# Macaron block with mixture of experts and windowed attention: both ends of the program anew (small weights turned by TensorE, loads in order of use, gates of the two outer passes spread by TensorE, idle matmuls in TensorE's waits there)

## The reference

```python
def ffn(X):                                   # on layernorm(x)
    shared = silu(X @ sW1 + sb1) @ sW2 + sb2  # 256 -> 128 -> 256
    logits = X @ routing_W.T + expert_bias    # 8 experts
    act = sqrt(softplus(logits))
    cf = the two largest of act in each row, 0 elsewhere
    hdn = silu(einsum('nd,edh->enh', X, rW1) + rb1[:, None])
    y = einsum('enh,ehd->end', hdn, rW2) + rb2[:, None]
    return shared + einsum('ne,end->nd', cf, y)
def attn(X):                                  # 16 heads of 16 channels
    q, k, v = heads(X @ Wq), heads(X @ Wk), heads(X @ Wv)
    # each token sees itself and the 63 before it
    return merge(softmax(q . k_window / 4) . v_window) @ Wo
x = x + 0.5 * ffn(layernorm(x))
x = x + attn(layernorm(x))
x = x + 0.5 * ffn(layernorm(x))
```

## Time and profile before

| | |
|---|---|
| time, median of 3 runs | 1589.93 us (1588.89 to 1590.38) |
| profiled execution, its own time | 1584.86 us |
| its span | 1583.1 us |
| mean granted clock of TensorE | 0.973 |
| TensorE busy | 1479.5 us, 93% |
| VectorE, ScalarE, POOL busy | 75%, 71%, 49% |

### The profile page before, as it was taken

How to read it: one execution, slowest core, us unless ns; L and a number is a source line. 1 busy time by engine, 2 the same in 40 slices (tenths; PEclk the granted TensorE clock), 3 DMA queues, 4 the chain that set the end, 5 groups by cost and what they waited for, 6 DMA issues and landing times.

```text
span 1583.1 us, 40702 instructions
## 1 busy us (share of the span) xinstructions
PE 1479.5 (93%) x13632; PEld 1333.7 (84%) x13632; DVE 1179.6 (75%) x4771; ACT 1128.6 (71%) x3400; POOL 779.8 (49%) x789
## 2 busy tenths in 40 slices
PE   2888999999999999999999999999999999998967
PEld 1777889898898989899898989989898988987756
DVE  5747677878878787887878787787878788675643
ACT  3358686877878687777878677787868778766823
...
GB/s 116 64 164 106 174 111 177 121 125 137 122 172 95 192 110 138 129 124 161 121 181 102 155 128 116 157 124 180 95 176 121 126 138 107 173 82 161 82 20 67
DMA packets 269957, 203.86 MB, mean 129 GB/s; under 512 B 154379, under 2 KB 224421, under 8 KB 269749
## 3 DMA queue, kind: packets, MB, share of 16 engines
...
q10 hardware_dynamic: 3408, 0.02, 0.1%
...
## 4 chain that ended last, share of the span: by engine, by line
PE 85%; DVE 5%; issue 3%; SPq 2%; DMA 2%; POOL 1%; ACT 1%; ACTq 0%; POOLq 0%; DVEq 0%
PE gb L937 12%; PE gb L939 11%; PE gb L938 11%; PE yb L937 9%; PE yb L939 8%; PE yb L938 8%; PE ptb L1000 7%; PE sb_ L991 6%; PE cxb L1019 4%; PE gb L1029 2%; PE gb L1041 2%; PE gb L1039 2%; PE gb L947 1%; SPq L479 1%; PE yb L1073 1%
## 5 line engine op out<-in xcount | busy, mean ns | idle before, releaser
L563 POOL TENSOR_TENSOR gl<-ag,gh 128x512 fp32r<-128x512 f32 x288 | 379.9, 1320 | 240.3 <-ACT gh L661 239.7
L546 POOL TENSOR_TENSOR pr<-pr,rinv 128x512 f32<-128x512 f32 x256 | 272.2, 1064 | 300.2 <-DVE rinv L822 298.3
L617 ACT ACTIVATE pr<-pr,mx 128x128 f32<-128x128 f32 x1024 | 397.5, 395 | 9.7 <-DVE mx L814 7.0
L937 PE MATMUL yb<-w2h,gh 128*128 128x256 f32 x1152 | 336.8, 292 | 12.4 <-POOL gl L563 12.3
L938 PE MATMUL yb<-w2h,gl 128*128 128x256 f32 x1152 | 324.0, 281 | 0.0
L939 PE MATMUL yb<-w2l,gh 128*128 128x256 f32 x1152 | 324.0, 281 | 0.0
L669 ACT ACTIVATE tt<-gb,b1half 128x512 f32<-128x512 f32 x288 | 195.4, 683 | 153.3 <-PE gb L939 147.7
L814 DVE CUSTOM_DVE_ANT_0 pr<-sb_,mask 128x128 f32<-128x128 f32 x1024 | 235.2, 285 | 53.8 <-issue 34.5
L881 DVE SCALAR_TENSOR_TENSOR ag<-gb,b,gate 128x512 f32<-128x512 f32 x256 | 188.2, 744 | 83.0 <-ACT tt L669 63.2
L661 ACT ACTIVATE gh<-ag 128x512 fp32r<-128x512 f32 x288 | 180.7, 628 | 95.1 <-DVE ag L887 66.8
L937 PE MATMUL gb<-xh,w1h 128*128 128x512 f32 x576 | 243.4, 423 | 2.6 <-DVE ag L881 2.0
...
## 6 DMA issues: line engine op xcount, KB each, us to landing
gate<-gates_pair SPq DMA_DIRECT2D x256, 256.0 KB, 3.7
ks<-qk_dram SPq DMA_DIRECT2D x256, 128.0 KB, 3.0
qs<-qk_dram SPq DMA_DIRECT2D x512, 64.0 KB, 2.6
...
```

Source lines behind the costliest of these rows:

```text
L546: nc.gpsimd.tensor_tensor(pr[:, k], pr[:, k], rinv[:, k, :].unsqueeze(2).to_broadcast([P, NP, P]), ALU.mult).then_inc(a_pn, 1)
L563: nc.gpsimd.tensor_tensor(gl[:, k, :], ag[:, k, :], gh[:, k, :].bitcast(F32), ALU.subtract).then_inc(f_gl, 1)
L617: nc.scalar.activation(pr[:, k, r, :], pr[:, k, r, :], ACT.Exp, bias=mx[:, k, r:r + 1], scale=-1.0, accum_out=rsum[:, k, r:r + 1]).then_in ...
L937: nc.tensor.matmul(dst, ah, bh, start=start, stop=False, **kw)
```

## The change

It has six parts.

1. *Small weights.* The router weights and first-layer biases come in rows, contiguous, to a tile `small` (in the tile that later holds `x2`), and three TensorE transposes (`Wt`) turn them. VectorE and ScalarE read the result from PSUM.
2. *Loads.* The order of the loads is changed, `1r` and `2r` are split by halves into `1r`, `1t` and `2r`, `2t`, the raw tiles are others, and POOL does not wait for the transfer of its mask any more.
3. *Clearing.* `Wz` goes from VectorE to POOL, behind the second `gl`.
4. *Gates of pass p of block 0 and of pass q of block 15.* A matmul `B` with a selector column spread over 128 columns writes an expert's gates to all partitions of a PSUM bank (`sb_` or `ptb`), and ScalarE copies them to `gate` (`K`). `cr`, `G1` and the eight `sp` are not run in these passes.
5. *Idle matmuls.* `Z24` is 24 products of the identity with itself, written to `cxb` and read by nobody. 159 such stand in TensorE's table at both ends.
6. *Tables.* `HEAD` now reaches from block 0 to 3, `TAIL` starts at block 10, and `ORDER` is changed between `qH2` and `pH0`. It has the same steps as before.

```diff
@@ step tables, start and end of TensorE's lists @@
 HEAD = {
     "PE": """
-pX0=0 pX1=0 pL=0 pH0=0 pC=0 pY0=0 pH1=0 pH2=0 pH3=0 pH4=0 pH5=0 pY1=0 pH6=0 pY2=0 pH7=0 pY3=0 pH8=0 pY4=0
+Wt=0 Z24=0 pX0=0 pX1=0 Z6=0 pL=0 pH0=0 pH1=0 pH2=0 Z19=0 pC=0 Z2=0 pB0=0 pB1=0 Z3=0 pB2=0 pH3=0 pB3=0 pB4=0
+pY0=0 pH4=0 pB5=0 pB6=0 pY1=0 pH5=0 pB7=0 pH6=0 pY2=0 pY3=0 pH7=0 pH8=0 pY4=0 pY5=0 pX0=1 pX1=1 pY6=0 pY7=0
+pL=1 pH0=1 pY8=0 Z29=1 pY0=1 aX0=0 aX1=0 Z4=1 pC=1 Z2=0 Q00=0 Q01=0 V0=0 pH1=1 pH2=1 Q10=0 Q11=0 V1=0 pY1=1
...
     "POOL": """
-prs=0 prs=1 pzz0=0 pgl0=0 pgl1=0 pgl2=0 pgl3=0 pgl4=0 pgl5=0 pgl6=0 pgl7=0 pgl8=0 pzz0=1 rsa=0 pgl0=1 prs=2
+prs=0 pzz0=0 pgl0=0 pgl1=0 Wz=0 pgl2=0 pgl3=0 prs=1 pgl4=0 pgl5=0 pgl6=0 pgl7=0 pgl8=0 rsa=0 pgl0=1 pzz0=1
...
     "SP": """
-LX=0 LX=1 LW2r=0 LW2s=0 LWvo=0 LW1s=0 LWqk=0 LW1r=0 LWb2=0 pG1=0 psp0=0 psp1=0 psp2=0 psp3=0 psp4=0 psp5=0
+LX=0 LW1s=0 LW1r=0 LW2s=0 LW2r=0 LX=1 LWb2=0 LWvo=0 LWqk=0 LX=2 pG1=1 psp0=1 psp1=1 psp2=1 psp3=1 QW0=0
@@ @@
+        small = x2.rearrange("p t d -> p (t d)")[0:NE, 0:KC * P + HID]
+        turned = sb_[:, :, :].rearrange("p r k -> p (r k)")
+        by_pe = {("p", 0), ("q", B - 1)}
+        def spread_to(m):
+            return sb_[:, :, :].rearrange("p r k -> p (r k)") if m % 2 == 0 else ptb[:]
@@ POOL @@
+            select(sel32[:], ALU.not_equal, 1.0, -32, [[-1, E]], 1)
+            select(sel32[:], ALU.not_equal, 1.0, -40, [[-1, E]], 1)
             pool.dma_start(mask[WIN:2 * WIN, :, :], mask[0:WIN, :, :]).then_inc(w_mask, 16)
-            pool.wait_ge(w_mask, 16)
+                if s == "Wz":
+                    nc.gpsimd.memset(qs[:].bitcast(F32), 0.0).then_inc(w_zero, 1)
+                    pool.wait_ge(w_lo, max(lo_done("1r"), lo_done("1t")))
+                    nc.gpsimd.memset(va[:], 0.0).then_inc(w_zero, 1)
@@ ScalarE @@
-            for c in range(KC):
-                act.dma_start(rwf[:, c, :], routing_w[:, c * P:(c + 1) * P].rearrange("e p -> p e"),
-                              allow_slow_non_contiguous=True).then_inc(w_in[0], 16)
+            act.dma_start(small[0:E, 0:KC * P], routing_w).then_inc(w_small, 16)
+            act.dma_start(small[0:1, KC * P:], sb1.rearrange("(a p) -> a p", a=1)).then_inc(w_small, 16)
+            act.dma_start(small[1:NE, KC * P:], rb1).then_inc(w_small, 16)
...
+                elif s[1] == "K":
+                    n, m = nth(s, b), int(s[2])
+                    act.wait_ge(f_gpe, E * (s[0] == "q") + m + 1)
+                    wait(act, f_a, NE * (n - 1) + m + 6 if m < 4 else NE * n + m - 2)
+                    nc.scalar.activation(gate[:, m % 4, :], spread_to(m), ACT.Copy).then_inc(f_gk, 1)
@@ VectorE @@
-                        dve.wait_ge(f_gate[m], 32 * n + 16 * ((e - 1) // 4) + 16)
+                        if (s[0], b) in by_pe:
+                            dve.wait_ge(f_gk, E * (s[0] == "q") + e)
+                        else:
+                            dve.wait_ge(f_gate[m], 32 * ns(s, b) + 16 * ((e - 1) // 4) + 16)
@@ TensorE @@
+                if s[0] == "Z":
+                    for _ in range(int(s[1:])):
+                        nc.tensor.matmul(cxb[:, 0:2, :].rearrange("p w q -> p (w q)"), ident[:], ident[:], start=True, stop=True)
+                elif s == "Wt":
+                    pe.wait_ge(w_small, 48)
+                    for c in range(KC):
+                        nc.tensor.transpose(turned[:, c * E:(c + 1) * E], small[0:E, c * P:(c + 1) * P], ident[0:E, 0:E])
+                    nc.tensor.transpose(turned[:, KC * E:KC * E + NE], small[:, KC * P:], ident[0:NE, 0:NE]) \
+                        .then_inc(w_smt, 1)
...
+                elif s[1] == "B":
+                    n, m = nth(s, b), int(s[2])
+                    if m == 0:
+                        pe.wait_ge(w_sel, 1)
+                        pe.wait_ge(f_cth, n + 1)
+                    if m > 1:
+                        pe.wait_ge(f_gk, E * (s[0] == "q") + m - 1)
+                    nc.tensor.matmul(spread_to(m), sel[:, m:m + 1].to_broadcast([P, P]), cft[:], start=True, stop=True) \
+                        .then_inc(f_gpe, 1)
```

More of the change, by code:

```diff
@@ new lines @@
+pH5=2 S0=1 pY2=2 pY3=2 S1=1 qX0=0 qX1=0 S2=1 P0=1 qL=0 S3=1 pH6=2 P1=1 pH7=2 S4=1 P2=1 pH8=2 U1=1 qH0=0 S5=1
+P3=1 pY4=2 U3=1 S6=1 pY5=2 P4=1 S7=1 pY6=2 P5=1 pY7=2 qC=0 U5=1 S8=1 P6=1 S9=1 P7=1 pY8=2 U7=1 qH1=0 qH2=0
+qH3=0 pX0=3 qY0=0 pX1=3 P8=1 S10=1 qY1=0 S11=1 aX0=2 aX1=2 pL=3 S12=1 qY2=0 Q00=2 Q01=2 qY3=0 P9=1 qH4=0
+P10=1 U9=1 S13=1 qH5=0 qH6=0 P11=1 Q10=2 S14=1 qH7=0 P12=1 U11=1 S15=1 qY4=0 V0=2 P13=1 qH8=0 P14=1 Q11=2
+qY5=0 P15=1 qY6=0 pH0=3 qY7=0 S0=2 qY8=0 pC=3 U13=1 U15=1 S1=2 V1=2 pY0=3 S2=2 P0=2 O0=1 S3=2 pH1=3 P1=2
@@ new lines @@
+Q01=12 pL=13 qH5=10 qY4=10 qH6=10 Q10=12 P12=11 qH7=10 V0=12 qH8=10 qY5=10 qY6=10 pC=13 P13=11 Q11=12 pH0=13
+P14=11 U13=11 S0=12 qY7=10 P15=11 qY8=10 S1=12 U15=11 V1=12 S2=12 pY0=13 P0=12 O0=11 S3=12 pH1=13 P1=12
+O1=11 S4=12 pH2=13 U1=12 pH3=13 S5=12 P2=12 pY1=13 pH4=13 pH5=13 P3=12 qX0=11 pY2=13 qX1=11 S6=12 U3=12
+pY3=13 P4=12 S7=12 qL=11 pY4=13 pY5=13 pH6=13 pH7=13 P5=12 pH8=13 qH0=11 U5=12 S8=12 P6=12 pY6=13 qC=11
+P7=12 S9=12 pY7=13 qH1=11 pY8=13 S10=12 qH2=11 pX0=14 U7=12 P8=12 S11=12 qY0=11 pX1=14 P9=12 qH3=11 qH4=11
@@ new lines @@
+pY7=14 pY8=14 S10=13 P7=13 qH1=12 qH2=12 pX0=15 S11=13 qY0=12 P8=13 qH3=12 U7=13 P9=13 pX1=15 qY1=12 aX0=14
+S12=13 P10=13 U9=13 qY2=12 aX1=14 qH4=12 P11=13 S13=13 qY3=12 Q00=14 Q01=14 S14=13 P12=13 pL=15 qH5=12
+qY4=12 qH6=12 P13=13 Q10=14 S15=13 P14=13 qH7=12 U11=13 qY5=12 V0=14 Q11=14 qH8=12 qY6=12 pC=15 pH0=15 S0=14
+P15=13 qY7=12 S1=14 U13=13 U15=13 V1=14 qY8=12 S2=14 P0=14 pH1=15 O0=13 pY0=15 S3=14 P1=14 O1=13 U1=14 S4=14
+P2=14 pH2=15 pH3=15 pH4=15 P3=14 pY1=15 S5=14 pH5=15 pH6=15 qX0=13 pY2=15 S6=14 qX1=13 U3=14 P4=14 pY3=15
@@ L171 @@
+qsp5=14 qsp6=14 qsp7=14 OUT=14 OUT=15
 """,
@@ L355, in split, with ns @@
             return pa[:, 2:4].rearrange("p w k n -> p (w k n)"), x1[1].rearrange("p t d -> p (t d)")
+        by_pe = {("p", 0), ("q", B - 1)}
+        def ns(s, b):
+            return sum(x not in by_pe for x in passes[:nth(s, b)])
         def wait(eng, s, value):
@@ L365, in run @@
             apart_ = set(head + tail)
+            apart_ |= {(x + k, b) for x, b in by_pe for k in ["G1", "cr"] + ["sp%d" % m for m in range(E)]}
             for s, b in head:
@@ L467, in step @@
                     c, hf = int(s[2]), int(s[3])
+                    if b == 0 and c == 0:
+                        sp.wait_ge(w_zero, 5)
                     if hf == 0:
@@ L631, in step @@
                     act.wait_ge(f_rstd, 4 * n + 4)
-                    wait(act, f_g1, 16 * n)
+                    wait(act, f_g1, 16 * ns(s, b))
                     src = xin[b % NXI] if s[0] == "p" else x2
@@ L1050, in step @@
                     mm.then_inc(f_ct, 1)
+                elif s[1] == "B":
[7 more added lines that the diff above has]
+                        .then_inc(f_gpe, 1)
                 elif s[1] == "H":
                     e, n, q = int(s[2]), nth(s, b), "pq".index(s[0])
-                    weights("1s" if e == 0 else "1r", n == 0 and e < 2)
+                    weights("1s" if e == 0 else "1r" if e == 1 else "1t", n == 0 and e in (0, 1, 1 + E // 2))
                     if e == 0:
@@ L1063, in step @@
                     k = (NE * n + e) % NG
-                    weights("2s" if e == 0 else "2r", n == 0 and e < 2)
+                    weights("2s" if e == 0 else "2r" if e == 1 else "2t", n == 0 and e in (0, 1, 1 + E // 2))
                     pe.wait_ge(f_gl, NE * n + e + 1)
```

385 lines of the change are left out of this document (223 added, 162 removed).

## The result

The changed kernel takes 1565.3 us (median of 4 runs, 1562.21 to 1570.2) against 1590.16 of the kernel before on the same chips (1588.89 to 1591.15): ratio 0.9847, 95% interval 0.9817 to 0.9877. Forecast were 1566. The profiled execution takes 1562.98 us with a span of 1561.1, so 22.0 less than before's 1583.1; the sum had said 24. The total is right and its parts are not: one term of 8.4 us is missing, and 11.3 us (6.4 net of what the blocks ahead of it pay) came from a place that I had put at 2.

What follows compares the result with a forecast made beforehand. The prediction took TensorE to bound the middle, with waits at both ends. Start 16, middle 0 and end 8 sum to a gain of 24 us: 1566 us in timed runs (1561 profiled), range 1556 to 1581.

Steps and rivals of the forecast that it cites:

- Bound and middle: Middle blocks: TensorE work end to end, period stays 91.04 us a block under the new table, gain 0.
- Start, term 1, the first transpose: Kernel start: earlier statistics bring the first transpose from 21.27 to 13.5 us, gain 7.8 (4.5 to 10).
- Start, term 2, the first pass: First pass of block 0: less VectorE work and gates without DRAM shorten it from 53.9 to 45.5 us, gain 8.4.
- From there TensorE is the limit: First pass, behind expert 2's product: TensorE work alone sets the remaining time, 17.3 us.
- Start in sum: Whole start, first transpose plus first pass: gain 16.2 us, taken as 16.
- a start of sixteen us that does not last: Sign of a wrong forecast: the start's sixteen us do not last to the middle, more idle between 109 and 230.
- End, 1430 to 1490: Before the last pass: gates of block 14 asked for earlier; of 10.5 us idle, 2 gained (0 to 5).
- rival C: Tables of blocks 0 to 3 and 10 to 15 remove most idle there: 10 to 15 us more, chance 0.13.
- Last pass: Last pass: upper clock level gives 2.1, gates without DRAM 3.5, one moved step 0.35; sum 6.0 us.
- D: Rival, both ends: idle matmuls never reach the upper level and delay steps behind them; 1597 us, chance 0.03.
- E: Rival, middle: the new table adds a wait, 1.9 us a block eats all the gain; 1590 us, chance 0.04.
- B: Rival, start: first-pass gain partly given back through slow clearing, late idle matmuls, late weights; gain 8 to 16, chance 0.20.

Runs made afterwards that it cites:

- e1: The changed kernel without its 159 idle matmuls, nothing else different: 1572.36 us, ratio 0.9892.
- e12: The changed kernel with the early clearing on POOL (e3) and 14 idle matmuls instead of 24 ahead of the first transposes: 1558.8 us, ratio 0.9836.
- e3: The changed kernel with both clearings on POOL moved, qs to behind the first inverse deviation and va to behind the fourth gl: 1563.55 us, ratio 0.9832.
- e2: The changed kernel with the gates of the two outer passes taken through DRAM again: 1572.0 us, ratio 0.9886.
- e11: The kernel before with only the idle matmuls of the last pass added: 1584.22 us, ratio 0.9976.
- e9: The changed kernel itself measured once more, nothing changed: 1566.55 us, ratio 0.9875.
- e6: The changed kernel with the steady and last tables of before, so only the new start: 1584.78 us, ratio 0.9973.
- e5: The kernel before with only the new table of blocks 10 to 15, without idle matmuls or spread gates there: 1583.3 us, ratio 0.9966.

## Why the prediction was right, point by point

**Bound and middle.** Right that TensorE bounds the blocks from 2 to 12: twelve of them took 1095.1 instead of 1092.4 us, gain 0 forecast, −2.7 found. But this small number is two larger ones. The steady table gave 2.2 us up to T q9, and the last table, which begins at block 10, cost 4.9 behind it; the period became uneven.

**Start, term 1, the first transpose.** Right: 5.31 and 13.20 where 5.3 and 13.5 stood, 8.07 gained of 7.8 forecast, and 11.40 without idle matmuls (e1) where 11.3 stood. The idle matmuls began at 5.92 instead of "near 6.5" and ran at the lower level until 9.9, so their 7.4 us were a bit more than the 7.0 forecast. Right also that they stand in the way: e12 gives 1.8 us of that back.

**Start, term 2, the first pass.** This term failed: 0.7 us gained, 8.4 forecast. The failing sentence is "From there TensorE is the limit", behind expert 2's product, whose time was met within 0.1 us. 17.3 us were forecast from there to the end of the pass (the terms add up to 17.2), 24.8 measured (41.47 to 66.31); 3.4 of the difference are the two waits, and 2.9 the two layers at the lower level. I had priced the clearing only as POOL's time and asked who waits for POOL. The question left out was who shares something with POOL: a VectorE step of 0.28 us took 4.17, and everything behind it on VectorE came late, the activation at 42.85, then the fourth gl at 44.28, then the bank that TensorE wanted, and then TensorE's level fell (e3 takes 4.2 us of this away, and its granted clock is 1.00 over the whole pass where the changed kernel's is 0.94). Of the Trainium skill, "SBUF — State Buffer", section "SBUF: two separate sides", in the notes on its diagram, says that a port pair shared by VectorE and GpSimd is an exclusive lock, held for the whole instruction, and that VectorE takes part in it with an operation in a 2-port mode, or, against a GpSimd operation that reads SBUF, with one that has two SBUF inputs. By that rule, the trace agrees in that not every VectorE operation is held: the `ag` at 35.39, which reads one input from PSUM, took its usual 0.74 us inside the memset, while the multiplication was held. Whether that one runs in a 2-port mode, no run here shows. The trace also goes further: the step began at 36.11, inside the first memset, and ended at 40.28, when the second one too was over (40.13). I had weighed the Trainium skill's rule on GpSimd's speed instead ("GPSIMD Engine Reference", section 8, Key points), and that one the trace contradicts for a memset: 3.52 us on POOL, 3.47 on VectorE. The gates' part of the term was about 3 us (e2: T p0 3.1 later through DRAM), not the 10.9 by which expert 1's product was to come earlier and the 9.1 by which it did, since other work bounds the rest of the pass.

**Start in sum.** 16 forecast; 9.0 in the pair of profiles, and 7.8 in the pair with the late T q0 (268.00 in e11, 260.16 in e9). As medians, e6 gives 4.6 for the start alone, behind the loss where the old table meets it. The prediction had named a start of sixteen us that does not last as a sign that it is wrong, and by this sign its mechanism for the start is: the store of block 0 came 9.0 us earlier, not sixteen.

**End, 1430 to 1490.** 2 forecast; the stretch from T q12 to T q14 gave 11.3. The range 0 to 5 looked only at idle time in a window. What moved was work, 110 records, out of a stretch in which the engines of two passes no longer fill TensorE, most of it into one that was full and became 4.9 us longer; e5 shows the table alone doing it, at a net of 4.4 to 6.1, and the pair of profiles gives 6.4. Of these 6.4, 2.4 are idle time; the rest is less busy time, 32 small records of it moved behind T q14 and the others presumably at the higher level (the granted clock of the window rose from 0.94 to 0.96), which no run separates. That was rival C's mechanism, at C's place (blocks 10 to 15) and in half of C's size. I gave it 0.13, too little, because I took C as all or nothing.

**Last pass.** 6.0 forecast, 4.4 found, with the shares turned round. The level was worth 2.35 (transposes and router products, forecast 2.1) and another 1.66 behind them, which I had not counted: the first layers, the shared expert's product and the gate transpose ran at the upper level too. The gates were worth 1.36 at expert 1's product, forecast 3.5. TensorE had H1 to H3 to do before the first spreading product (1528.22 to 1532.4), so part of the trip to DRAM had lain beside work; that this is the whole reason is argued, not tested. 0.6 of it goes again in the rest of the pass, and 0.3 before the transposes.

**Rivals.** D (idle matmuls at the lower level) did not occur: 0.23 us each at the upper level, as the row of a 128x512 product suggested; only part of the first 24 ran at the lower one. E did not occur. B's outcome, a first pass that gives back what it gains, is what happened, though not by the two causes that it names for this pass: the clearing took 5.3 us, not 7.7, and the idle matmuls ended at 13.2, not 16.8. C made up for it. Against the sum of 24 the start fell short by 7.0 and the last pass by 1.6, the steady blocks gave 2.2 more and the stretch from T q9 to T q14 4.4 more than its 2, which leaves 22.0: the point was hit by errors that cancel, and that is luck.
